# Self attention in a fused transformer kernel: from masked copies of the keys over 96 and 112 rows to one head per 32-partition row tile

## The chip, the cores and the metric

The kernel runs on one core of one Trainium2 chip. The metric is device time in microseconds (us) of one execution, median of several; lower is better. TensorE is written PE (its weight loads PEld), VectorE DVE, ScalarE ACT, GpSimd POOL, SyncE SP.

## What is computed

The reference runs four layers, each an attention and a feed-forward block, over x of 4 batches x 512 tokens x 128 channels. The change touches the last layer's self attention (16 heads of 8 channels, full 512 x 512, no mask), which stands in the fourth feed-forward block ahead of its routed experts:

```
h = layernorm(y)*g + b                        # y: 512 x 128 of one batch
q, k, v = h @ wq + bq, h @ wk + bk, h @ wv + bv
p = softmax(q_h @ k_h.T / sqrt(8))            # for each head h of 16, 512 x 512
y = y + concat_h(p @ v_h) @ wo + bo
then a layernorm, a router (top 1 of 8) and eight experts of 128 -> 512 -> 128
```

## The kernel before

One program drives five engines. For every engine a function (`tensor`, `scalar`, `vector`, `gpsimd`, `sync`) holds generators of the same names, and `order` (from L2350) interleaves the same streams in the same way for all five: `weave` advances the stream whose next piece has the earliest fractional time. Each engine executes its own list strictly in that order; semaphores (`Signal`, waits through `Waits`) tie the lists together. So a wait that stands in an engine's list holds back all that is behind it. PSUM has 8 banks of 512 words; `Banks.take` hands out banks of a ring, and the user of a bank waits for the reader of its last use.

The self attention (loop at L2403) has 16 units s, one for each batch b = s // 4 and group g = s % 4 of four heads. In turn i of 18 the streams are `first(i)`, `second(i-1)` and `third(i-2)`:

- `first` projects queries and keys of one group. The weights hold the 32 columns of the group three times, so a projection of 96 rows gives three copies. ACT adds the bias and rounds to float32r (L1134, L1118), DVE subtracts to get the low parts for one of the copies (L1500, L1486). With three copies (high, low, high against high, high, low) a float32r product keeps nearly float32 accuracy. Then DVE and ACT write four masked copies of the keys, 112 rows each (L1493, L1125, two each), so that a product over all rows sees one head alone.
- `second` finds the maximum of each query over its 512 keys: for 4 query blocks t and 2 head pairs, two products over 96 rows into banks 0 to 3 and one DVE reduction over two banks (L1884), 8 a unit. Four transposes (L516) turn the maxima into rows, DVE copies them (L1513), and SP moves them by one DMA (L2197) into rows 96 to 111 of the queries.
- `third` makes the scores transposed (keys on partitions) over 112 rows, the maximum subtracted through its row: 16 products with banks 4 to 6 as ring, 16 exponentials on ACT (L1325), and 4 groups of value products (`values`, 128 rows x 32 columns, four at a time, float32) into bank 7, copied to OT by DVE (L1897).

`third(s)` starts with `w.wait_ge(*mq[par].at("s", s))`, the landing of the maxima. Beside the units run `self_norms(b+1)` (two layernorms, the transposed and scaled h, values; turns 2, 6, 10), `tail4` (division by the sums, output projection; turns 6, 10, 14), `route3` (router, same turns) and `place3(0)` (slots of the experts; turn 11). All small pieces of these streams take their banks from the ring of 4 to 6 as well.

## Time and profile before

| | |
|---|---|
| median of 3 runs | 1301.2 us (1296.91 to 1304.37) |
| the profiled execution | 1300.78 us, its span 1299.0 us |
| PE, DVE, ACT, POOL busy | 1063.6, 691.8, 445.7, 139.2 us |
| mean granted TensorE clock | 0.875 |
| self attention, from the first raw products to the last output copy | about 821 to 1184 us of the span |

Busy time of an engine is the time in which it had at least one instruction under way; matmuls are pipelined, so their durations overlap. The granted clock is a share of full speed: 1.00 is 2.4 GHz, 0.50 is 1.2 GHz. A rate in brackets behind a timeline row is the idle time before it and who ended it.

### The profile page before, as it was taken

The numbers are of one execution on the slowest core, as the hardware profiler recorded it, in microseconds if no ns is written. First come the engines' busy times: TensorE is split into PE (matmuls) and PEld (weight loads), VectorE is DVE, ScalarE is ACT, GpSimd is POOL, SyncE is SP. The second block draws the span as 40 slices with busy tenths as digits, with TensorE's granted clock in tenths as the row PEclk, the third lists the DMA queues.
The fourth block names the chain that finished last, engine by engine and source line by source line (L and its number), as shares of the span: only waits on it lengthen the run. The fifth ranks groups of instructions, "written<-read, shape, count | busy, mean of one in ns | idle before, by whom it ended". The sixth has DMA issues, their size and how long they took to land.

```text
span 1299.0 us, 14949 instructions
## 1 busy us (share of the span) xinstructions
PE 1063.6 (82%) x5592; PEld 594.4 (46%) x5592; DVE 691.8 (53%) x1741; ACT 445.7 (34%) x834; POOL 139.2 (11%) x135
## 2 busy tenths in 40 slices
PE   4688999999977773875988888789789789898983
PEld 2244566665533332652753333344444444444753
DVE  5345656554554533327434434777767767673532
ACT  2334333232132220112223223356446336354431
POOL 1000000000001112015210001000100120000222
PEclk7889999999986865996888899789889879789987
DMA  9500000000210000121000000000000000001122
GB/s 297 161 1 1 1 1 1 1 1 1 77 54 1 7 6 27 44 65 25 2 6 1 1 1 1 2 2 3 2 3 3 2 17 3 1 2 33 41 62 71
DMA packets 31216, 33.34 MB, mean 26 GB/s; under 512 B 4037, under 2 KB 22621, under 8 KB 31144
## 3 DMA queue, kind: packets, MB, share of 16 engines
q1 hardware_dynamic: 29096, 28.59, 7.2%
q0 software_dynamic: 2048, 3.79, 1.1%
q8 instruction: 45, 0.74, 0.2%
q14 instruction: 27, 0.22, 0.1%
HBM read 22.53 MB, written 9.70 MB: 25 GB/s over the span
## 4 chain that ended last, share of the span: by engine, by line
PE 67%; DVE 21%; issue 5%; ACT 3%; POOL 2%; DMA 1%; SPq 0%; POOLq 0%; DVEq 0%; ACTq 0%
PE PS L170 61%; DVE MX L1884 5%; DVE KB L1555 3%; PE PS L634 2%; DVE KB L1493 1%; DVE Ht L1422 1%; DVE st L1409 1%; DVE OT L1596 1%; PE PS L1020 1%; PE PS L516 1%; DVE STG L1486 1%; POOL OT L2096 1%; PE PS L642 1%; POOL ve L2079 1%; DVE CX L1596 1%
## 5 line engine op out<-in xcount | busy, mean ns | idle before, releaser
L1325 ACT ACTIVATE PT<-PS 128x512 f32<-128x512 f32 x256 | 140.9, 596 | 114.1 <-PE PS L170 112.3
L1884 DVE TENSOR_REDUCE MX<-PS 128x2 fp32r<-128x1024 f32 x128 | 151.9, 1218 | 14.2 <-PE PS L170 13.2
L1220 ACT ACTIVATE PT<-PS 77x512 f32<-77x512 f32 x192 | 98.0, 590 | 158.5 <-PE PS L170 158.5
L170 PE MATMUL PS<-CX 32*77 32x512 f32 (+2 forms) x896 | 128.0, 579 | 18.9 <-DVE OT L1596 7.8
L170 PE MATMUL PS<-HT,RA 128*128 128x512 f32 x288 | 131.6, 599 | 0.0
L170 PE MATMUL PS<-KB,QB 96*128 96x512 f32 x256 | 102.5, 494 | 25.4 <-DVE MX L1884 23.3
L2079 POOL TENSOR_TENSOR ve<-ve,nh 128x4 f32<-128x4 f32 x40 | 41.4, 1036 | 699.6 <-DVE ve L1417 699.6
L170 PE MATMUL PS<-QB,KB 112*128 112x512 f32 x256 | 107.6, 473 | 3.0 <-ACT PT L1325 2.3
L1555 DVE TENSOR_REDUCE KB<-PS 128x16 fp32r<-128x1232 f32 x48 | 69.1, 1439 | 70.7 <-PE PS L170 70.4
L170 PEld LDWEIGHTS PS<-RA,PT 128*128 128x128 f32 x816 | 98.8, 193 | 16.2 <-issue 16.2
L170 PE MATMUL PS<-RA,PT 128*128 128x128 f32 (+1 forms) x816 | 102.8, 277 | 1.5 <-DVE PT L2006 1.2
L1254 ACT ACTIVATE PT<-PS 128x512 f32<-128x512 f32 x72 | 42.9, 597 | 127.7 <-PE PS L170 127.7
L170 PE MATMUL PS<-HT,S 128*96 128x512 f32 (+1 forms) x104 | 71.5, 782 | 14.2 <-DVE KB L1555 10.9
L170 PEld LDWEIGHTS PS<-KB,QB 96*128 96x128 f32 x256 | 48.0, 212 | 74.5 <-DVE MX L1884 48.6
L1723 DVE TENSOR_TENSOR PT<-PT,PS 128x512 f32<-128x512 f32 x72 | 49.5, 687 | 57.0 <-PE PS L170 48.1
L170 PEld LDWEIGHTS PS<-CX 32*128 32x128 f32 (+1 forms) x896 | 48.1, 191 | 66.7 <-issue 21.5
L170 PEld LDWEIGHTS PS<-HT,RA 128*128 128x128 f32 x288 | 52.3, 192 | 54.2 <-issue 53.3
L170 PE MATMUL PS<-PT,RB 128*32 128x512 f32 x512 | 71.8, 654 | 0.0
L170 PEld LDWEIGHTS PS<-QB,KB 112*128 112x128 f32 x256 | 49.9, 202 | 47.1 <-ACT PT L1325 35.5
L170 PE MATMUL PS<-PT,VB 77*32 77x512 f32 x384 | 57.7, 677 | 6.1 <-ACT CX L1168 3.2
L170 PE MATMUL PS<-KB 32*77 32x512 f32 x192 | 53.9, 960 | 0.0
L170 PE MATMUL PS<-RB,PT 128*128 128x128 f32 (+2 forms) x352 | 49.8, 303 | 4.2 <-DVE PT L1580 3.3
(236 smaller groups left out, 1363.5 us busy)
## 6 DMA issues: line engine op xcount, KB each, us to landing
RA<-in_l_w SPq DMA_DIRECT2D x1, 2304.0 KB, 11.0
RB<-in_l_w SPq DMA_DIRECT2D x1, 2048.0 KB, 14.2
RA<-in_l_w SPq DMA_DIRECT2D x1, 2048.0 KB, 8.7
d<-OT SPq DMA_DIRECT2D x2, 960.0 KB, 7.9
RB<-d SPq DMA_DIRECT2D x6, 256.0 KB, 3.1
o<-PT SPq DMA_DIRECT2D x6, 256.0 KB, 2.3
dbuf<-OT SPq DMA_DIRECT2D x2, 640.0 KB, 4.9
X<-in_x SPq DMA_DIRECT2D x4, 256.0 KB, 4.5
```

The lines of the kernel that those rows point to most:

```text
L170: return e.matmul(o, l, r, start=first, stop=last, skip_group_check=True)
L516: m = e.transpose(PS[0:M.shape[2], k, 128 * t:128 * t + 128], M[:, t, :].bitcast(F32), ident[:, :])
L634: m = e.transpose(PS[:, k, 128 * hg:128 * hg + 128], outputs_at(key, hg)[:, 128 * j:128 * j + 128], ident[:, :])
L642: m = e.transpose(PS[:, k, 128 * j:128 * j + 128], ON[:, 256 * j + 128 * c:256 * j + 128 * c + 128], ident[:, :])
L1220: e.activation(slot[s][0:NK, :], PS[0:NK, 4 + j, :], ACT.Exp, bias=0.0, scale=a.scale).then_inc(*expd(i, r, j))
L1254: e.activation(slot[s], PS[:, banks.of(silu, i, x, c), :], ACT.Silu).then_inc(*silu(i, x, c))
L1325: e.activation(slot[p], PS[:, banks.of(expd, "s", s, c, j), :], ACT.Exp, bias=0.0, scale=a4.scale).then_inc(*expd("s", s, c, j))
L1555: e.tensor_reduce(o, PS[:, 0:4, 0:308].rearrange("p i (r k) -> p i r k", k=NK), AX, ALU.max).then_inc(*rmax(i, t))
L1596: e.tensor_copy(outputs_at((i,), r), PS[:, 0, :]).then_inc(*otc(i, r))
L1723: e.tensor_tensor(P, P, PS[:, banks.of(glu, i, x, c), :], ALU.mult).then_inc(*glu(i, x, c))
L1884: e.tensor_reduce(Mv[par][:, t, RM + 4 * g + 2 * p2:RM + 4 * g + 2 * p2 + 2], PS[:, 2 * p2:2 * p2 + 2, :], AX, ALU.max).then_inc(*rmax("s" ...
L2079: e.tensor_tensor(ve[:, 8 * par + 4:8 * par + 8], ve[:, 8 * par:8 * par + 4], nh[:, :], ALU.pow).then_inc(*rstd(*key))
```

## The change

Each head of a group gets a row tile of 32 partitions: rows 0 to 7 of the tile hold the high part, 8 to 15 the low part, 16 to 23 the high part again (for the keys high, high, low), and row 24 the maximum (against -1 in the keys). So no masked copies are needed, and a product of one head uses 32 rows.

- Queries and keys of all 16 heads are projected once per batch, in `self_norms` (two 128 x 512 products), and split into high and low there (ACT, then DVE with 128 x 512). `first` puts the rows of a group in place with selector matrices (two accumulating float32r products over 128 rows for the queries, two for the keys), each followed by one ACT copy (QS, KS). The selectors are loaded (1 MB) and rounded once by POOL, after turn 21 of the earlier units.
- `second`: products over 32 rows, the two of a pair on neighbouring row tiles, into a pair of banks out of 0 to 3 (`take_pair`); the maxima are 16 columns, one transpose, one ACT copy of 16 x 128, and SP moves them by four DMAs of one row each.
- `third`: scores over 32 rows with banks 4 to 6; everything else now takes banks of 0 to 3. The output copy goes from DVE to ACT, one unit later in its list.
- `tail4`, `route3` and `place3(0)` are placed otherwise: `route3` in turns 7, 11, 15, `place3(0)` in turn 13.

```diff
@@ tensor: self_norms
+                for n, wt in enumerate((a4.wq, a4.wk)):
+                    k, free = banks.take(qsplit, "n", b, n)
+                    w.wait_ge(*free)
+                    mm(e, PS[:, k, :], wt, HTv[par]).then_inc(*projected("n", b, n))
+                    yield
@@ tensor: first
-                yield from queries(a4, ("s", b), b % 2, g, hT.at("s", b))
-                yield from keys(a4, s, g, 512, HTv[b % 2])
+                w.wait_ge(*pinit.at("sel"))
+                for n, (N, done) in enumerate(((QN[b % 2], qact), (KNv[b % 2], kact))):
+                    k, free = banks.take(done, "s", s)
+                    w.wait_ge(*free)
+                    w.wait_ge(*qsplit.at("n", b, n))
+                    mm(e, PS[:, k, :], SELm[:, 2 * n, g, :], N[0], True, False)
+                    mm(e, PS[:, k, :], SELm[:, 2 * n + 1, g, :], N[1], False, True).then_inc(*(kproj if n else projected)("s", s))
+                    yield
@@ tensor: second
-                        for j in range(2):
-                            k = 2 * p2 + j
-                            w.wait_ge(*banks.take_at(k, rmax, "s", s, t, p2))
-                            m = mm(e, PS[:, k, :], QQ[par][0:RM, 512 * g + 128 * t:512 * g + 128 * t + 128], kv[0:RM, 2 * p2 + j, :])
+                        k, frees = banks.take_pair(rmax, "s", s, t, p2)
+                        for free in frees:
+                            w.wait_ge(*free)
+                        for j in (2 * p2, 2 * p2 + 1):
+                            m = mm(e, PS[:, k + j % 2, :], Q[32 * j:32 * j + 32, 128 * t:128 * t + 128], K[32 * j:32 * j + 32, :])
                         m.then_inc(*raw("s", s, t, p2))
                         yield
-                yield from maxima(("s", s), Mv[par], rmax.at("s", s, 3, 1))
+                k, free = banks.take(mts, "s", s)
+                w.wait_ge(*free)
+                w.wait_ge(*rmax.at("s", s, 3, 1))
+                e.transpose(PS[0:16, k, 0:128], MXs[s % 2].bitcast(F32), ident[:, :]).then_inc(*mxT("s", s))
@@ tensor: third, scores
-                        k, free = banks.take(expd, "s", s, c, j)
-                        w.wait_ge(*free)
-                        mm(e, PS[:, k, :], kv[0:RK, j, 128 * c:128 * c + 128], QQ[par][0:RK, 512 * g:512 * g + 512]).then_inc(*scored("s", s, c, j))
+                        k = 4 + (4 * c + j) % 3
+                        w.wait_ge(*banks.take_at(k, expd, "s", s, c, j))
+                        mm(e, PS[:, k, :], K[32 * j:32 * j + 32, 128 * c:128 * c + 128], Q[32 * j:32 * j + 32, :]).then_inc(*scored("s", s, c, j))
@@ scalar: first, second, third
+                e.activation(QS[s % 4], PS[:, banks.of(qact, "s", s), :], ACT.Copy).then_inc(*qact("s", s))
+                e.activation(KS[s % 4], PS[:, banks.of(kact, "s", s), :], ACT.Identity, bias=a4.minus, scale=1.0).then_inc(*kact("s", s))
+                w.wait_ge(*mxT.at("s", s))
+                e.activation(MTs[s % 2][0:16, :], PS[0:16, banks.of(mts, "s", s), 0:128], ACT.Copy).then_inc(*mts("s", s))
+                    e.activation(OT[:, 512 * g:512 * g + 512], PS[:, 7, :], ACT.Copy).then_inc(*ots("s", b, g))
@@ sync: second
-                e.dma_start(QQ[par][RM:RK, 512 * g:512 * g + 512].bitcast(F32), MT[RM:RK, :].bitcast(F32)).then_inc(*mq[par]("s", s))
+                for j in range(4):
+                    e.dma_start(QS[s % 4][32 * j + 24:32 * j + 25, :].rearrange("o (t q) -> o t q", t=4).bitcast(F32),
+                                MTs[s % 2][4 * j:4 * j + 4, :].bitcast(F32)).then_inc(*mq[s % 2]("s", s))
@@ order
-                    streams.append((first(i), 12))
+                    streams.append((first(i), [0.1, 0.16]))
-                    streams.append((second(i - 1), 11))
+                    streams.append((second(i - 1), [0.12 * n for n in range(9)]))
-                    streams.append((tail4((i - 6) // 4), 36))
+                    streams.append((tail4((i - 6) // 4), 14, 0.3))
-                if i in (6, 10, 14):
-                    streams.append((route3((i - 6) // 4), 22, 0.4))
-                if i == 11:
+                if i in (7, 11, 15):
+                    streams.append((route3((i - 7) // 4), 26))
+                if i == 13:
```

How the lists of two engines change is shown at two places. First PE, where a unit's maxima are transposed and the next unit's scores begin, in a turn without other streams. L516 and L883 are the transposes of the maxima; KB,QB are raw products, QB,KB scores, PT,RB value products, HT,S the old query projection, QB,RR the new selector products. Before:

```order
L516 MATMUL PS<-ident,MX 112x128 [waits rmax,expd]
L516 MATMUL PS<-ident,MX 112x128 x3
L170 MATMUL PS<-QB,KB 128x512 [waits expd] x2
L170 MATMUL PS<-PT,RB 32x512 x4
L170 MATMUL PS<-PT,RB 32x512 [waits expd]
L170 MATMUL PS<-PT,RB 32x512 x3
L170 MATMUL PS<-HT,S 96x512
L170 MATMUL PS<-KB,QB 128x512 [waits kcD,kcA]
L170 MATMUL PS<-KB,QB 128x512 x3
L170 MATMUL PS<-QB,KB 128x512 [waits mq0]
```

Now:

```order
L177 MATMUL PS<-PT,RB 32x512 x4
L177 MATMUL PS<-PT,RB 32x512 [waits expd]
L177 MATMUL PS<-PT,RB 32x512 x3
L883 MATMUL PS<-ident,KB 16x128 [waits rmax]
L177 MATMUL PS<-KB,QB 128x512 [waits mts]
L177 MATMUL PS<-KB,QB 128x512
L177 MATMUL PS<-QB,RR 128x512 x2
L177 MATMUL PS<-QB,KB 128x512 [waits mq1]
L177 MATMUL PS<-KB,QB 128x512 [waits qact]
```

The transpose moved behind the last value products of the unit before, and one pair of raw products instead of two stands between it and the first score.

Second ACT at the same place (L1302 and L1325 are the exponentials, L1293 the copy of the maxima, L1282 and L1286 the copies of queries and keys, L1309 the output copy). Now:

```order
L1302 ACTIVATE PT<-PS 128x512 [waits scored] x3
L1293 ACTIVATE KB<-PS 16x128 [waits mq1,mxT]
L1282 ACTIVATE QB<-PS 128x512 [waits projected]
L1302 ACTIVATE PT<-PS 128x512 [waits scored,weighed]
L1302 ACTIVATE PT<-PS 128x512 [waits scored]
L1286 ACTIVATE KB<-PS,cols 128x512 [waits kproj]
L1302 ACTIVATE PT<-PS 128x512 [waits scored] x2
L1309 ACTIVATE OT<-PS 128x512 [waits weighed]
L1302 ACTIVATE PT<-PS 128x512 [waits scored] x4
```

Before, in the like turn:

```order
L1325 ACTIVATE PT<-PS 128x512 [waits scored,weighed]
L1325 ACTIVATE PT<-PS 128x512 [waits scored]
L1118 ACTIVATE STG<-PS,cols 96x512 [waits kcA,kcD,kproj]
L1325 ACTIVATE PT<-PS 128x512 [waits scored] x2
L1325 ACTIVATE PT<-PS 128x512 [waits scored,weighed]
L1125 ACTIVATE KB<-STG,msk 112x512 [waits ksplit]
L1125 ACTIVATE KB<-STG,msk 112x512
L1325 ACTIVATE PT<-PS 128x512 [waits scored] x3
```

The copy of the maxima and the output copy are new in ACT's list; the copies of the keys' mask are gone.

## Rows read from the trace of the kernel before

**Rows 1.** Groups by line, 861.7 to 1183 us: engine, count, busy, mean, idle before.
```profile
L1884 DVE TENSOR_REDUCE MX<-PS 128x2 fp32r<-128x1024 f32 x112 | 132.7, 1218 | 11.5 <-PE PS L170 10.7
L1325 ACT ACTIVATE PT<-PS 128x512 f32<-128x512 f32 x240 | 131.9, 597 | 103.0 <-PE PS L170 101.4
L170 PE MATMUL PS<-QB,KB 112*128 112x512 f32 x240 | 100.3, 471 | 3.0 <-ACT PT L1325 2.3
L170 PE MATMUL PS<-KB,QB 96*128 96x512 f32 x224 | 87.1, 480 | 17.9 <-DVE MX L1884 17.9
```

**Rows 2.** Stretches: length, busy PE, PEld, DVE, ACT, POOL, clock, DMA share, GB/s.
```profile
815.00:861.70 46.70, 34.61 (x120) 17.37 (x121) 34.94 (x62) 17.13 (x29) 3.47 (x3) 0.78 0.01 2
895.60:912.50 16.90, 15.60 (x73) 7.14 (x74) 13.08 (x14) 11.03 (x20) 0.00 (x0) 1.00 0.01 3
912.50:946.30 33.80, 25.66 (x124) 13.89 (x124) 25.23 (x72) 13.52 (x23) 5.76 (x5) 0.90 0.01 1
946.30:970.50 24.20, 20.98 (x89) 10.86 (x90) 14.79 (x21) 11.62 (x21) 0.00 (x0) 0.86 0.01 2
...
1039.30:1069.20 29.90, 25.14 (x91) 13.02 (x92) 19.85 (x42) 11.62 (x21) 8.68 (x8) 0.71 0.06 19
1103.10:1133.60 30.50, 26.43 (x112) 13.60 (x111) 18.87 (x41) 12.55 (x22) 2.31 (x2) 0.78 0.01 2
...
1157.90:1172.00 14.10, 13.70 (x69) 6.69 (x70) 10.56 (x10) 8.37 (x16) 0.00 (x0) 1.00 0.02 6
1172.00:1183.00 11.00, 10.16 (x49) 3.36 (x50) 0.69 (x1) 8.16 (x16) 0.00 (x0) 1.00 0.15 44
```

**Rows 3.** Timeline of the end of a turn without other streams: start, duration, what.
```profile
892.02 2.28 ACT L1325 ACTIVATE PT<-PS 128x512 f32<-128x512 f32 x4 [1.11 <-PE PS L170]
892.12 0.62 PE L516 MATMUL PS<-ident,MX 128*112 128x128 f32 x4
...
893.50 0.51 SPq L2197 DMA_DIRECT2D QB<-MT  x1
893.60 1.92 PE L170 MATMUL PS<-PT,RB 128*32 128x512 f32 x16
...
895.59 0.69 DVE L1897 COPY OT<-PS 128x512 f32<-128x512 f32 x1 [2.11 <-PE PS L170]
```

**Rows 4.** Groups by line, 860 to 1240 us: work of a unit beside reductions and exponentials.
```profile
L1125 ACT ACTIVATE KB<-STG,msk 112x512 fp32r<-112x512 f32 x26 | 17.2, 711 | 0.0
...
L1493 DVE TENSOR_SCALAR KB<-STG,msk 112x512 fp32r<-112x512 f32 x26 | 13.7, 570 | 0.3
...
L1513 DVE CAST MT<-PS 16x512 fp32r<-16x512 f32 x14 | 9.8, 697 | 10.0 <-PE PS L516 9.9
L1486 DVE SCALAR_TENSOR_TENSOR STG<-PS,cols,STG 32x512 fp32r<-32x512 f32 x13 | 9.7, 749 | 0.8 <-ACT STG L1118 0.4
```

**Rows 5.** Tile QB, 861 to 905 us: durations min, median, max in ns; landing of DMAs.
```profile
L170 PE MATMUL PS<-QB,KB x42: 389/397/645, 863.4 to 904.3; 112*128 112x512 f32 x42
...
DMA to landing us min/median/max: 1.9/1.9/1.9
```

**Rows 6.** Timeline of SP's queue: two issues with two others between them.
```profile
21.16 0.39 SPq L2176 DMA_DIRECT2D MT<-in_mbT  x1
...
22.35 0.33 SPq L2176 DMA_DIRECT2D off<-in_c_off  x1
```

**Rows 7.** Stretches of 3 us within a heavy turn, columns as in Rows 2.
```profile
929.00:932.00 3.00, 0.45 (x2) 0.00 (x1) 2.90 (x10) 2.30 (x4) 1.01 (x1) 1.00 0.00 0
932.00:935.00 3.00, 2.37 (x7) 1.58 (x7) 3.00 (x8) 0.10 (x1) 1.44 (x1) 0.52 0.00 0
```

**Rows 8.** Timeline: one group of value products at either clock.
```profile
885.57 1.07 PE L170 MATMUL PS<-PT,RB 128*32 128x512 f32 x8
...
937.63 1.69 PE L170 MATMUL PS<-PT,RB 128*32 128x512 f32 x8
```

**Rows 9.** Timeline: four float32r products of 32 rows in an earlier attention.
```profile
754.39 0.81 PE L170 MATMUL PS<-KB 32*77 32x512 f32 x4
```

More of the change, by code:

```diff
@@ L23 @@
 NT = 15
-RM = 96
-RK = 112
 GATE = 25
@@ L91, in again, with only @@
     def again(self):
-        self.order, self.ends = list(self.places), {}
-    def only(self, places):
-        self.order = list(places)
+        self.order, self.ends, self.paired = list(self.places), {}, False
+    def only(self, places, paired=False):
+        self.order, self.paired = list(places), paired
     def hold(self, k):
@@ L110, in take, with take_pair @@
     def take(self, signal, *key):
-        k = self.order.pop(0)
+        alone = [k for k in self.order if k ^ 1 not in self.order] if self.paired else []
+        k = (alone or self.order)[0]
+        self.order.remove(k)
         self.order.append(k)
         return k, self.take_at(k, signal, *key)
+    def take_pair(self, signal, *key):
+        k = [k for k in self.order if k ^ 1 in self.order][0] & 6
+        self.order = [x for x in self.order if x & 6 != k] + [k, k + 1]
+        frees = [self.take_at(k + n, signal, *key) for n in (1, 0)]
+        return k, frees
     def of(self, signal, *key):
@@ L180, in program @@
         KB = sb("KB", 3 * 2048, F32R)
+        with nc.sbuf_tensor("RR", [128, 8192], F32R) as RRt:
+            RR = RRt
         RB = sb("RB", 8192)
@@ L238, in program @@
         vall = VB[:, :].rearrange("p (b h c) -> p b h c", b=4, h=16)
-        Mv = [MX[:, 4 * RK * p:4 * RK * p + 4 * RK].rearrange("p (t c) -> p t c", t=4) for p in range(2)]
         W13 = RA[:, 0:9 * 512].rearrange("p (e n) -> p e n", e=9)
@@ L489, in prepare @@
                     banks.free(k)
-            def keys(a, n, g, cols_n, rhs):
-                k, free = banks.take(ksplit, n)
-                w.wait_ge(*free)
-                mm(e, PS[0:96, k, 0:cols_n], a.wk[:, g, :], rhs).then_inc(*kproj(n))
-                banks.hold(k)
-                yield from idle(2)
-                banks.free(k)
-                yield from idle(2)
-            def queries(a, key, par, g, ready):
-                k, free = banks.take(qsplit, *key, g)
-                w.wait_ge(*free)
-                w.wait_ge(*ready)
-                w.wait_ge(*ld[a.ready].all())
-                mm(e, PS[0:96, k, :], a.wq[:, g, :], HTv[par]).then_inc(*projected(*key, g))
-                banks.hold(k)
-                yield from idle(2)
-                banks.free(k)
-                yield
-            def maxima(key, M, ready):
-                k, free = banks.take(mtc, *key)
-                w.wait_ge(*free)
-                w.wait_ge(*ready)
-                for t in range(4):
-                    m = e.transpose(PS[0:M.shape[2], k, 128 * t:128 * t + 128], M[:, t, :].bitcast(F32), ident[:, :])
-                m.then_inc(*mxT(*key))
-                banks.hold(k)
-                yield
-                banks.free(k)
-                yield
             def front(i):
@@ L912, in values @@
                     if c == 0:
-                        w.wait_ge(*banks.take_at(7, otc, "s", b, g))
+                        w.wait_ge(*banks.take_at(7, ots, "s", b, g))
                         w.wait_ge(*vprep.at("s", b))
@@ L1054, in hook @@
                 elif name == "self":
-                    banks.only([4, 5, 6])
+                    banks.only(range(4), True)
                 elif name == "experts3":
@@ L1332, in third @@
                     yield
+                if s == 15:
+                    outputs(s)
             def tail4(b):
@@ L2126, in self_norms @@
                 add_row(Yb[b], 4, ("s", b))
-                yield
+                yield from idle(3)
             def tail4(b):
@@ L2164, in hook @@
                     gather(1)
+                elif name == "l3x1":
+                    w.wait_ge(*ld["l3sel"].all())
+                    e.tensor_copy(RR[:, 6144:8192], RB[:, 6144:8192]).then_inc(*pinit("sel"))
             nothing = lambda *a: none()
@@ L2282, in hook @@
                     w.wait_ge(*capV.at("o", 7))
-                    load("l3s", w4, A["l3s_w"])
+                    load("l3s", w4[:, 0:512], A["l3s_w"])
                 elif name == "l2m":
@@ L2289, in hook @@
                     load("c3", C3[:, 0:368], A["c_3"])
+                    w.wait_ge(*pe2.at(19, "down"))
+                    load("l3sel", RB[:, 6144:8192], A["l3_sel"])
             nothing = lambda *a: none()
@@ L2493 @@
         msk[:, 36 + n] = part // 16 == n
+    sel = _np.zeros((4, 4, 128, 128), _np.float32)
+    for g in range(4):
+        for j in range(4):
+            for k, places in enumerate(((0, 2), (1,), (0, 1), (2,))):
+                for n in places:
+                    for d in range(8):
+                        sel[k, g, 32 * g + 8 * j + d, 32 * j + 8 * n + d] = 1.0
     place8 = _np.arange(128).reshape(4, 4, 8).transpose(1, 0, 2).ravel()
```

201 lines of the change are left out of this document (69 added, 132 removed).

## The prediction

> **What bounds the kernel now.** I read the busy shares first (PE 1063.6 of 1299 us), then stretches turn by turn, then the timeline of one turn, because the average says nothing about this stage. The output copy of each unit (L1897) marks the turns. In a turn without other streams the stretch is 16.9 us [rows 2]: PE is busy 15.6 us of it, at full clock, DVE 13.1, ACT 11.0. I call this a plain turn; there are seven in the stage (3, 4, 5, 8, 9, 12, 13), all at 16.9 us. In the whole stage ACT idled 103 us ahead of its exponentials, 101.4 of it for PE [rows 1]. So plain turns are bound by PE's list. The heavy turns are another matter: turn 6, with two layernorms, the output tail and the router, lasts 33.8 us with DVE busy 25.2 and PE 25.7 [rows 2]; turn 7 lasts 24.2, turn 11 29.9, turn 14 30.5. There DVE's load and the waits between engines decide, and PE falls to the lower clock: after three microseconds with PE busy 0.45 us, the next three had a granted clock of 0.52, close to the 1.2 GHz level [rows 7].
>
> The change promises PE time: raw products and scores cost PE 87.1 and 100.3 us in this stretch [rows 1]. What replaces PE as the bound must be read from the order lists, and there I find a chain, below.
>
> **A plain turn after the change.** I walk from the first exponential of a unit to the first of the next.
>
> (a) ACT. Four exponentials back to back took 2.28 us [rows 3], so 16 take 9.1. Between them stand the copy KS and the output copy, 128 x 512 like an exponential (0.60 us mean, [rows 1]) and with a bias somewhat more: 1.3 together. The score bank ring has three banks, so ACT has up to three exponentials ahead while PE makes value products (1.07 us a group, [rows 8]), and a score product after them takes 0.40 [rows 5]; three exponentials are 1.7 us. That just covers it; I add 0.2 for joints. Sum 10.6 us. QS is copied in the pause (b).
>
> (b) The way back. By the order list all is serial now: last exponential of the unit, last value products (1.1 us), transpose of the maxima (0.35, from four in 0.62 [rows 3]), ACT's copy of 16 x 128 (0.3; bounds: 0.2 and the 0.70 of the 16 x 512 copy it replaces [rows 4]), SP's four DMAs, landing, the wait of the first score, the score itself (0.4), start of ACT (0.1). A DMA of this kind landed 1.9 us after its issue [rows 5]. Four issues of small loads in a row are 0.40 us apart (21.16 to 22.35 us holds three gaps, [rows 6]), so the last lands 1.2 + 1.9 = 3.1 us after the copy; with signals between engines 3.3. Sum: 1.1 + 0.35 + 0.3 + 3.3 + 0.5 = 5.55 us. In this time PE has one raw pair and one selector pair, under 1.2 us, and everything behind the score waits in its list: raw products too, so DVE gets one reduction of eight.
>
> Before, the transposes stood four scores, value groups and a projection ahead: the DMA left at 893.50 while PE still had the 1.92 us of values at 893.60 and raw products after them [rows 3], so it was covered. The one DMA, a copy on DVE and this cover are what the change gives up.
>
> (c) Together 10.6 + 5.55 = 16.2 us at full clock. DVE needs 13.1 less two masked copies (2 x 0.57), the transposed maxima 0.70, two splits (2 x 0.75) [rows 4] and the output copy 0.69 [rows 3], so 9.1 to 9.4 us: hidden. PE needs about 11: hidden too, but see the clock.
>
> (d) The clock. Over the last 3.6 us of the way back PE is busy about 1.1 us. [Rows 7] show such a lull followed by the 1.2 GHz level. There the value group took 1.69 instead of 1.07 us [rows 8], and the first score after it comes late by twice that and more, past the three exponentials in store: about 1.3 us for a chunk. If every lull is followed by some 6 us at the low level, one chunk and the first score are hit: +1.4 us, 17.6 us. If the whole turn runs there, two chunks (2.6), the last values (0.9 + 0.6) and the start: +4.5, 20.7 us. I take 17.6. The Trainium skill ("TensorE: Matmul & The Clock Gate", section "HAM oscillation") says that PE-idle gaps between bursts let the gate throttle again and that each burst then starts cold, which would make the 20.7 likelier than the 16.2; no row here shows this pattern for 32-row products.
>
> **The other turns**, before and after:
> - Turns 6, 10. DVE 25.2 us [rows 2], less 4.0 of the unit's work, less the router's layernorm that moves out (2.6), plus the two 128 x 512 splits of the batch (1.5): 20.1. DVE idled 8.6 of the turn before; now it must idle in the way back, 5.55 less one reduction, and a little for POOL. About 26 against 33.8: -15.6 for two.
> - Turns 7, 11, 15 (router). DVE about 14 to 14.6, again with a pause of 4.4 and joints: 20.5 against 24.2, 29.9 [rows 2] and, for 15, about 24.2: -16.8.
> - Turn 14 loses the router: 20 against 30.5 [rows 2]: -10.5.
> - Turn 13 is plain plus `place3` (about 20 small DVE pieces): 19 against 16.9: +2.1.
> - Six plain turns, 17.6 against 16.9: +4.2.
> - Turns 16 and 17 have no new raw products to hide and were short, 14.1 and 11.0 [rows 2]. They hold the same chain: 17 and 15: +6.9.
> - The start (turns 0 to 2, 46.7 us from 815, [rows 2]): no masks ahead of the first product, raw pairs on two row tiles so that DVE's reductions follow each other at 1.22, less DVE in turn 2, but two more projections and splits in `self_norms(0)`: -5, between -10 and 0.
> - Elsewhere: the selector load (1 MB) and POOL's rounding (about four times the 1.3 us of its 128 x 512 operations) have some 130 us until the first use, and POOL is 11% busy: 0. The experts start from the same point: 0.
>
> Sum: -15.6 - 16.8 - 10.5 + 2.1 + 4.2 + 6.9 - 5 = -34.7 us. The profiled execution took 1300.8, 0.4 under the median; 1266 us, which I give for both.
>
> **Rivals.**
> 1. *The clock stays high* or heavy turns shrink further. For: plain turns before ran at 1.00, and the pause is broken by a raw pair and selectors. Against: [rows 7]. It gives 16.2 in seven plain turns (-10) and 1 us less in nine others: about 1247.
> 2. *The whole stage at 1.2 GHz, slower than before.* The mechanism: every way back drops the clock, and at the low level value products (1.69, [rows 8]) outlast the exponentials in store, so that PE is thin and slow for the whole turn. Plain turns 20.7: +3.1 on seven, +2.5 on nine others: 1266 + 44 = 1310. It decides for slower from about 2 us a turn over my values. Against: PE dense again in each turn should bring the clock back, as it did within some 6 us after [rows 7].
> 3. *A longer way back*: four one-row DMAs cost more than 0.40 apart, or land later. 0.5 us more a step and 0.6 more landing give 1.5 + 0.6 = 2.1 us, of which turns 6 and 10 hide some: 14 x 2 = 28: 1294.
> 4. *Nothing gained*: the heavy turns keep their length because waits, not DVE work, made them (DVE idled 8.6 us there). Then -42.9 of the sum shrinks to some -10: about 1299.
> 5. *PE's saving comes through whole.* Four row tiles at once: four 32-row products took 0.81 us under way together [rows 9] where a 112-row one takes 0.40 alone [rows 5]. Three quarters of 87.1 + 100.3 us [rows 1] are 141 us: 1160. The Trainium skill ("TensorEngine Tiling (Array Packing)", section "Theoretical Speedup") puts up to 4x on products of 32 rows or fewer, which is this sum. Against: the scores are fed one by one by exponentials of 0.57 us, and the pause in (b) is not PE work. That the change makes no 32-row tiles is excluded by its operands.
>
> **How the numbers follow.** Forecast as summed (1250 to 1283): 0.50. Rival 1: 0.22. Rival 3: 0.12. Rival 2: 0.08. Rival 4: 0.06. Rival 5: 0.02. Half a per cent (6.5 us), about what a measurement of this kernel can tell from no change, puts the lines at 1294.7 and 1307.7. Faster: 0.50 + 0.22 + 0.02 + a good half of rival 3 and a little of 4, 0.83. Within: the rest of 3 and 4 and some of rival 2, 0.09. Slower: 0.08. The range takes in rivals 1, 3 and 4: 1236 to 1300; the unknown prices (DMA spacing, ACT's small copy, the start) fit in it. The predicted time is the forecast's.
>
> **What would show it.** Right: plain turns 16 to 18 us between output copies, in each a stretch near 5.5 us where ACT does only the small copy and QS, PE's first score waiting for the DMA; reductions waiting for PE; granted clock dipping behind each pause; PE busy well under 1063 us; turn 6 about 26 us. Wrong: plain turns near 12 us would mean the pause is covered; over 19 us, rival 2 or 3, told apart by the granted clock and by the time from the small copy to the landing; turn 6 still over 31 us, rival 4.

## The result and the profile after

The changed kernel took 1374.72 us (median of 4 runs, 1366.99 to 1383.11) against 1302.78 for the kernel before (median of 4 runs, 1296.91 to 1309.14): a ratio of 1.055, 95% interval 1.046 to 1.065. It is slower by 5.5%. The forecast was 1266 us, its range 1236 to 1300, and slower had a chance of 0.08. The profiled execution took 1367.5 us, its span is 1364.9 against 1299.0 before, so 65.9 us have to be found.

The page of the changed kernel: its busy line and the granted clock in 40 slices. The mean clock is 0.784 (0.875 before).

```profile
PE 1097.2 (80%) x5560; PEld 573.9 (42%) x5560; DVE 638.1 (47%) x1651; ACT 441.1 (32%) x842; POOL 140.4 (10%) x136
...
PEclk7799999999977757968887896757556655757987
```

PE has 33.6 us more busy time (1063.6 before), though the products of this stage are smaller, and the slices of the self attention, from the 26th to the 37th, read 5 to 7.

The groups by line from 869.2 to 1250.5 us, which answer to [rows 1] (columns as there):

```profile
L1836 DVE TENSOR_REDUCE KB<-PS 128x2 fp32r<-128x1024 f32 x110 | 134.0, 1225 | 155.4 <-PE PS L177 155.3
L1302 ACT ACTIVATE PT<-PS 128x512 f32<-128x512 f32 x237 | 127.7, 600 | 144.0 <-PE PS L177 143.4
L177 PE MATMUL PS<-QB,KB 32*128 32x512 f32 x236 | 113.7, 725 | 39.8 <-DMA QB<-KB 31.2 <-ACT PT L1302 8.6
L177 PE MATMUL PS<-PT,RB 128*32 128x512 f32 x480 | 104.9, 990 | 0.3 <-ACT PT L1302 0.3
L177 PE MATMUL PS<-KB,QB 32*128 32x512 f32 x220 | 94.8, 692 | 11.5 <-ACT KB L1293 4.6 <-DVE rt L1856 3.0 <-DVE KN L1822 1.1
```

DVE and ACT work as long as before on each reduction and exponential (1225 and 600 ns against 1218 and 597), and wait longer, for PE. A mean score product (QB,KB) lasts 725 ns where the 112-row product took 471, a mean raw product (KB,QB) 692 where the 96-row product took 480. The value products, which the change does not touch, went from a mean of 650 to 990 ns; their line in the kernel before, 861.7 to 1183 us:

```profile
L170 PE MATMUL PS<-PT,RB 128*32 128x512 f32 x480 | 66.7, 650 | 0.0
```

The wait for the DMA of the maxima is there too, 31 us in the whole stage; the experiments below tell how much of the loss it makes.

The stretches between output copies (now L1309 on ACT), columns as in [rows 2]: the start, two plain turns (3 and 4), turns 6, 7, 11, 14, 15, 16, 17 and the experts behind them.

```profile
815.00:869.20 54.20, 39.48 (x158) 18.65 (x154) 32.64 (x64) 18.56 (x34) 3.29 (x3) 0.71 0.00 1
869.20:891.30 22.10, 19.53 (x73) 6.32 (x70) 9.86 (x9) 10.42 (x22) 0.00 (x0) 0.50 0.01 1
891.30:913.30 22.00, 18.65 (x71) 5.99 (x69) 9.72 (x9) 10.32 (x22) 0.00 (x0) 0.58 0.00 0
934.60:967.90 33.30, 25.89 (x117) 12.20 (x116) 19.10 (x49) 14.20 (x27) 4.57 (x4) 0.76 0.00 1
967.90:1000.60 32.70, 26.58 (x97) 11.52 (x96) 12.38 (x21) 11.20 (x23) 0.00 (x0) 0.50 0.00 1
1077.10:1109.80 32.70, 26.54 (x97) 11.57 (x97) 12.28 (x21) 11.15 (x22) 0.00 (x0) 0.50 0.00 1
1153.80:1183.70 29.90, 22.68 (x101) 10.31 (x100) 14.66 (x30) 12.12 (x23) 2.32 (x2) 0.73 0.01 1
1183.70:1215.50 31.80, 24.01 (x93) 10.47 (x93) 12.62 (x21) 9.79 (x20) 0.00 (x0) 0.55 0.00 1
1215.50:1236.70 21.20, 15.98 (x60) 4.79 (x59) 6.85 (x6) 8.95 (x19) 0.00 (x0) 0.58 0.08 25
1236.70:1250.50 13.80, 12.13 (x44) 2.81 (x44) 0.00 (x0) 6.73 (x14) 0.00 (x0) 0.50 0.00 1
1250.50:1364.90 114.40, 82.74 (x508) 61.32 (x508) 44.51 (x140) 34.97 (x88) 26.58 (x26) 0.90 0.18 54
```

A plain turn takes 22.0 us where it took 16.9, with the clock at 0.50 to 0.58, that is at the 1.2 GHz level for nearly all of it. ACT's and DVE's busy times, 10.4 and 9.8 us, are near what the forecast had. What changed is PE: it is busy 18.7 to 19.5 us, where the forecast had about 11.

Stretches of 3 us inside one such turn, same columns:

```profile
894.30:897.30 3.00, 2.69 (x16) 0.84 (x15) 1.04 (x1) 1.41 (x3) 0.00 (x0) 0.50 0.00 0
897.30:900.30 3.00, 3.00 (x14) 0.66 (x13) 1.32 (x2) 0.95 (x3) 0.00 (x0) 0.50 0.00 0
900.30:903.30 3.00, 2.69 (x13) 0.89 (x15) 2.45 (x2) 1.78 (x4) 0.00 (x0) 0.50 0.00 0
903.30:906.30 3.00, 2.64 (x15) 0.47 (x7) 0.00 (x0) 0.27 (x1) 0.00 (x0) 0.60 0.00 0
906.30:909.30 3.00, 0.98 (x4) 0.30 (x2) 1.23 (x1) 0.60 (x1) 0.00 (x0) 0.97 0.01 3
909.30:912.30 3.00, 2.67 (x8) 1.08 (x8) 1.23 (x1) 1.77 (x3) 0.00 (x0) 0.50 0.00 0
```

The second row is what the forecast did not foresee: PE is busy 3.00 of 3.00 us and the clock is at 0.50. The clock comes up in the pause, right behind the 16 value products, and is down again when the next unit begins. These rows alone do not say whether the pause or the products after it bring the clock down; the experiments have to. The Trainium skill ("TensorE: Matmul & The Clock Gate", section "What's actually happening") says that the gate is set by how busy PE has been recently. If busy is read as the profile's busy time, this row speaks against it.

The timeline of the same turn's end (start, duration, what):

```profile
897.25 1.94 PE L177 MATMUL PS<-PT,RB 128*32 128x512 f32 x8
...
901.80 3.64 PE L177 MATMUL PS<-PT,RB 128*32 128x512 f32 x16
905.37 0.38 PE L883 MATMUL PS<-ident,KB 128*16 128x128 f32 x1
906.11 0.50 PE L177 MATMUL PS<-KB,QB 32*128 32x512 f32 x2 [0.36 <-ACT KB L1293]
906.54 0.73 PE L177 MATMUL PS<-QB,RR 128*128 128x512 f32 x2
909.59 0.79 PE L177 MATMUL PS<-QB,KB 32*128 32x512 f32 x1 [2.32 <-DMA QB<-KB]
909.60 0.80 PE L177 MATMUL PS<-KB,QB 32*128 32x512 f32 x2
...
910.32 1.22 PE L177 MATMUL PS<-KB,RR 128*128 128x512 f32 x2
```

The value group takes 1.94 us (1.07 at full clock, [rows 8]). SP's four DMAs were issued from 906.09 on, and the first score, at 909.59, waits for the last of them, as foreseen. Two raw products on neighbouring row tiles took 0.80 us together at the low level, about as long as one alone, where a pair over 128 rows took 1.22.

### The profile page after: what moved, and what is told of

It is laid out like the page before. It is cut to its first block, busy times and chain, and to the rows that moved or that the text cites. A ratio compares the mean times of both kernels' runs of the same rounds, so it can differ in the third digit from the quotient of the medians.

```text
span 1364.9 us, 14813 instructions
## 1 busy us (share of the span) xinstructions
PE 1097.2 (80%) x5560; PEld 573.9 (42%) x5560; DVE 638.1 (47%) x1651; ACT 441.1 (32%) x842; POOL 140.4 (10%) x136
## 4 chain that ended last, share of the span: by engine, by line
PE 69%; DVE 13%; ACT 5%; issue 5%; DMA 3%; POOL 2%; SPq 2%; POOLq 0%; ACTq 0%; DVEq 0%
PE PS L177 62%; DVE KB L1505 3%; PE PS L608 3%; ACT PT L1302 2%; SPq L2142 2%; DMA QB<-KB 2%; DVE KB L1836 1%; DVE Ht L1407 1%; DVE OT L1546 1%; POOL ve L2021 1%; PE PS L1008 1%; DVE st L1394 1%; POOL OT L2038 1%; DVE CX L1546 1%; PE PS L616 1%
## 5 line engine op out<-in xcount | busy, mean ns | idle before, releaser
L1836 DVE TENSOR_REDUCE KB<-PS 128x2 fp32r<-128x1024 f32 x128 | 155.6, 1224 | 169.9 <-PE PS L177 169.7
L1302 ACT ACTIVATE PT<-PS 128x512 f32<-128x512 f32 x256 | 138.1, 599 | 154.5 <-PE PS L177 153.8
L177 PE MATMUL PS<-QB,KB 32*128 32x512 f32 x256 | 122.9, 719 | 43.8 <-DMA QB<-KB 35.1
L177 PE MATMUL PS<-KB,QB 32*128 32x512 f32 x256 | 107.8, 689 | 18.0 <-ACT KB L1293 5.3
L177 PE MATMUL PS<-PT,RB 128*32 128x512 f32 x512 | 110.7, 980 | 0.3 <-ACT PT L1302 0.3
L177 PEld LDWEIGHTS PS<-QB,KB 32*128 32x128 f32 x256 | 51.1, 277 | 137.5 <-issue 53.7
L177 PEld LDWEIGHTS PS<-KB,QB 32*128 32x128 f32 x256 | 41.9, 273 | 35.6 <-ACT KB L1293 9.1
L177 PE MATMUL PS<-HT,S 128*128 128x512 f32 x56 | 42.8, 865 | 15.5 <-DVE KB L1505 10.8
```

What stands on the lines that cost most here:

```text
L177: return e.matmul(o, l, r, start=first, stop=last, skip_group_check=True)
L1302: e.activation(slot[p], PS[:, banks.of(expd, "s", s, c, j), :], ACT.Exp, bias=0.0, scale=a4.scale).then_inc(*expd("s", s, c, j))
L1836: e.tensor_reduce(o, PS[:, k:k + 2, :], AX, ALU.max).then_inc(*rmax("s", s, t, p2))
```

## The experiments

Two theories ran through the first four runs. Theory A is the forecast's mechanism: the pause in each way back lowers the clock. Theory B, called N in the later runs: products that use only 32 rows leave the clock low even where PE is busy without a gap. The kernel before, run on the same chips, took 1303.3 to 1307.5 us. Runs without an interval are single executions.

**The pause covered.** The second stream begins its steps earlier, so that the transpose stands before the last score and two value groups.

```
-    streams.append((second(i - 1), [0.12 * n for n in range(9)]))
+    streams.append((second(i - 1), [0.1 * n for n in range(9)]))
```

> The changed kernel with the raw products of a unit placed at 0.1 n of a turn instead of 0.12 n, so that the transpose of the maxima stands before the last score and two value groups. The changed kernel's plain turn is 22.0 us, of which the pause from the last values to the first score is about 4.2 us. Theory A (the pause both costs its own length and drops the clock): the pause is covered, plain turns fall to 13 to 16 us with a granted clock of 0.9 or more in them, the kernel to 1250 to 1290 us. Theory B (32-row products do not bring the clock up, whatever stands between them): the pause goes, but the granted clock stays near 0.5, plain turns 17.5 to 19 us, kernel 1315 to 1340 us.

It took 1351.5 us. PE no longer waits for the DMA of the maxima. Six of the seven plain turns were 20.5 to 21.4 us at a clock of 0.50 to 0.64, one was 16.7 at 0.81. The turn lost at most 1.5 us, not the clock's share: the direction of theory B, though slower than its figures (17.5 to 19 us, 1315 to 1340 us).

**The pause filled.** The two selector products for the queries are made four times, so that PE works with 128 rows in the pause.

```
+    for _ in range(FILL if n == 0 else 0):
+        mm(e, PS[:, k, :], SELm[:, 2 * n, g, :], N[0], True, False)
+        mm(e, PS[:, k, :], SELm[:, 2 * n + 1, g, :], N[1], False, True)
```

> The changed kernel with the two selector products of the queries made four times instead of once (same result), in the pause ahead of the first score, so that PE works there on all 128 rows. The order of everything else is kept. Theory A (the idle pause drops the clock): the clock stays or comes up, the value groups take 1.07 instead of 1.94 us, plain turns 17 to 18.5 us, kernel 1315 to 1335 us. Theory B (the 32-row products leave the clock low): the clock rises at most for the start of the unit and falls again; plain turns 20 to 22 us, kernel 1350 to 1375 us.

1377.2 us, plain turns 20.9 to 22.8 us at 0.57 to 0.67, slightly above theory B's figures in time. PE's wait for the DMA was down to 0.94 us in turns 4 and 5, and the first score behind it took 0.50 us, as at full clock, where the changed kernel's took 0.79. The mean clock of the turn rose by less than 0.1 for it: work over 128 rows in the pause does not hold the clock up through the unit.

**One DMA in place of four.**

```
-    for j in range(4):
-        e.dma_start(QS[s % 4][32 * j + 24:32 * j + 25, :]...)
+    e.dma_start(QS[s % 4][24:128:32, :].bitcast(F32), MTs[s % 2][0:16, :].bitcast(F32)).then_inc(*mq[s % 2]("s", s))
```

> The changed kernel with the four one-row DMAs of a unit's maxima as one DMA to partitions 24, 56, 88 and 120. The issues took 2.42 us for four; with one the landing comes 1.5 to 1.9 us earlier in each of 16 turns. If the way back is a serial chain: 24 to 30 us less, 1340 to 1350 us, and with a shorter lull perhaps a higher clock and more. If the landing is not what the first score waits for: no change, 1367 to 1383 us.

1355.9 us, some 12 us under the changed kernel's profiled run (the fastest but one of its four runs, which spread from 1367.0 to 1383.1), and half of the 24 to 30 us expected: plain turns 18.3 to 21.2 us, still at 0.50 to 0.72. So the way back is on the path, and its four issues cost about 0.6 us each, but it is a small part of the loss.

**A pause in the kernel before.** Its transposes are moved behind the last value products.

```
-    streams.append((second(i - 1), 11))
+    streams.append((second(i - 1), [n / 11 for n in range(9)] + [0.96, 0.97, 0.98]))
```

> The kernel before, with its four transposes of the maxima moved behind the last value group of the unit before, as in the changed kernel; nothing else is changed. It adds a pause of about 2.5 us (DMA of 1.9 us less the products in between). Theory A (a pause drops the clock): plain turns go from 16.9 to above 21 us with clock 0.5 to 0.7 in them, kernel 1345 us or more. Theory B (products over 96 and 112 rows hold the clock, only 32-row ones do not): plain turns 19 to 20 us at clock 0.95 or more, kernel 1325 to 1345 us.

1312.4 us against 1304.9 for the kernel before on that chip. Plain turns took 18.2 to 18.3 us (two 19.9) and kept a clock of 1.00 (those two 0.91). That is less than either theory had (19 to 20 us, or over 21), because the pause made was small: PE waits 1.05 to 1.12 us for the DMA, where the changed kernel's waits 2.3 in most plain turns. Such a pause costs 1.3 us a turn and lowers the clock in two of seven. It is a weak test of theory A; the next run has the full pause.

**Full rows in the changed kernel.** The next four runs change how many rows the products contract and, so that all values stay finite, the scale of the exponentials. They compute something else than the reference. In this one both kinds of products use all 128 rows.

```
-    ...Q[32 * j:32 * j + 32, 128 * t:128 * t + 128], K[32 * j:32 * j + 32, :])
+    ...Q[:, 128 * t:128 * t + 128], K[:, :])
-    ...K[32 * j:32 * j + 32, 128 * c:128 * c + 128], Q[32 * j:32 * j + 32, :])
+    ...K[:, 128 * c:128 * c + 128], Q[:, :])
-    ...ACT.Exp, bias=0.0, scale=a4.scale)
+    ...ACT.Exp, bias=0.0, scale=0.01 * a4.scale)
```

> Leaves the computation changed: the raw and score products contract all 128 rows (the four heads of a tile at once), with the exponentials' scale cut to a hundredth so that all stays finite; the number of instructions, their columns and their order are the changed kernel's. Theory N (the granted clock follows the rows that the products use, so that products of 32 rows alone leave it at 1.2 GHz even where PE is busy without a gap): plain turns at a granted clock of 0.90 to 1.00 and 16.5 to 18.5 us long, 1265 to 1300 us in all. Rival O (the clock stays low for the order of the work or its waits, not for its rows): the clock stays at 0.50 to 0.60, plain turns 21 to 22.5 us, 1360 to 1380 us.

1312.3 us, beside 1307.5 for the kernel before on the same chip: 55 us under the changed kernel's profiled run (62 under its median), most of the loss. A plain turn and its 3 us stretches, in this run:

```profile
889.96:906.93 16.97, 13.96 (x70) 7.03 (x69) 9.68 (x9) 10.40 (x21) 0.00 (x0) 1.00 0.00 0
...
892.00:895.00 3.00, 3.00 (x20) 1.58 (x16) 1.82 (x3) 2.35 (x6) 0.00 (x0) 1.00 0.00 0
...
901.00:904.00 3.00, 0.71 (x3) 0.30 (x2) 1.23 (x1) 0.60 (x1) 0.00 (x0) 1.00 0.01 3
904.00:907.00 3.00, 2.64 (x12) 1.80 (x10) 1.31 (x2) 2.69 (x6) 0.00 (x0) 1.00 0.00 0
```

The way back is still there: PE is busy 0.71 of 3 us, and here the clock stays at 1.00 in it and after it. Five of the seven plain turns read 1.00. The other two do not:

```profile
906.93:925.16 18.23, 15.58 (x69) 8.11 (x68) 12.03 (x21) 10.53 (x21) 1.02 (x1) 0.85 0.01 1
...
1091.47:1111.29 19.82, 16.02 (x71) 8.13 (x69) 13.04 (x21) 10.52 (x21) 8.29 (x8) 0.83 0.08 27
```

In each a wait for the maxima (2.28 us in the first) is followed by three microseconds at 0.50. So it is in the turns with side streams: of the 14 waits from turn 3 on, five are followed by three microseconds at 1.00, nine by three at 0.50 to 0.77. Theory A's mechanism is there, then, and costs a plain turn 1.3 us when it strikes (18.23 for 16.97). But with full rows the clock comes back within the next turn, and with 32 rows it comes up for a few microseconds at most in nearly every turn; that is what keeps the changed kernel's turns low. Theory B's figures for the plain turn are met in five turns of seven, its total (1265 to 1300 us) is missed by 12 us. The raw and the score products, by duration in two turns of each kernel (minimum, median, maximum in ns), of the changed kernel:

```profile
L177 PE MATMUL PS<-KB,QB x34: 490/789/792, 868.5 to 912.3; 32*128 32x512 f32 x34
L177 PE MATMUL PS<-QB,KB x34: 623/788/792, 869.1 to 913.0; 32*128 32x512 f32 x34
```

and with all rows:

```profile
L177 PE MATMUL PS<-QB,KB x34: 388/396/503, 872.8 to 907.0; 128*128 128x512 f32 x34
...
L177 PE MATMUL PS<-KB,QB x32: 389/393/501, 873.5 to 906.5; 128*128 128x512 f32 x32
```

Four times the rows, half the time.

**Full rows in the scores alone, and in the raw products alone.** The second or the first of the two edits above, with the smaller scale in both.

> The score products alone contract all 128 rows, the raw products stay at 32; the exponentials' scale is cut to a hundredth. Scores are half of the narrow columns (16 products of 512 a turn) and lie beside the value products in ACT's stretch. Theory N: the clock is up in ACT's stretch and low in the raw stretch or in none: mean 0.75 to 1.00 in plain turns, 17 to 19.5 us, 1280 to 1325 us. Rival O: 0.50 to 0.60, 21 to 22.5 us, 1360 to 1380 us.

> The raw products alone contract all 128 rows, the scores stay at 32; the exponentials' scale is cut to a hundredth. Theory N: half way too, as with the scores alone: clock 0.70 to 1.00 in plain turns, 17 to 20 us, 1285 to 1335 us. Rival O: 0.50 to 0.60, 21 to 22.5 us, 1360 to 1380 us.

Scores alone: 1374.2 us, plain turns 19.3 to 26.4 us at 0.56 to 0.85. Raw products alone: 1429.7 us, 20.9 to 28.2 us at 0.56 to 0.83. Both missed theory B's half way figures in time, and the raw products' run is slower than the rival had it too. The clock did rise above the changed kernel's, for some turns, but not to stay. That these runs are slower than the changed kernel at a higher clock may come from 128-row products taking their full time at the low level where two 32-row products lie side by side; it was not tried apart. Both runs use the smaller scale of the exponentials and are slow, so that edit alone does not bring the clock back.

**32 rows in the kernel before.** The converse: its raw and score products cut to the first 32 rows, nothing else but the scale.

```
-    ...QQ[par][0:RM, ...], kv[0:RM, 2 * p2 + j, :])
+    ...QQ[par][0:32, ...], kv[0:32, 2 * p2 + j, :])
-    ...kv[0:RK, j, ...], QQ[par][0:RK, ...])
+    ...kv[0:32, j, ...], QQ[par][0:32, ...])
```

> The kernel before, its raw and score products cut from 96 and 112 rows to the first 32, so that they leave out most of each product (the maximum too; the exponentials' scale is cut to a hundredth); instructions, columns, order and waits are the kernel's before. Theory N: the clock falls to 0.50 to 0.65 in the plain turns, which then take 20 to 22.5 us, 1350 to 1400 us in all. Rival O: the clock stays at 0.95 to 1.00, plain turns 16.5 to 17.5 us, 1295 to 1310 us.

1405.9 us, theory B's direction and beyond its figures (1350 to 1400 us, plain turns of 20 to 22.5). Plain turns went from 16.9 us to 25.7 (one 23.4, one 20.3) at clocks of 0.56 to 0.83. All its narrow products lie on rows 0 to 31, so none can lie beside another on a different row tile. Four stretches of 3 us where the clock falls:

```profile
863.90:866.90 3.00, 2.61 (x9) 1.20 (x9) 2.00 (x3) 1.27 (x3) 0.00 (x0) 1.00 0.00 0
866.90:869.90 3.00, 3.00 (x10) 1.50 (x10) 2.97 (x3) 1.91 (x5) 0.00 (x0) 0.98 0.00 0
869.90:872.90 3.00, 3.00 (x10) 1.35 (x12) 2.51 (x4) 2.49 (x5) 0.00 (x0) 0.50 0.01 3
872.90:875.90 3.00, 3.00 (x12) 1.48 (x5) 2.17 (x4) 0.10 (x2) 0.00 (x0) 0.50 0.00 0
```

There is no pause as in the changed kernel, PE is busy 2.61 of 3 us and then throughout, and the clock drops to 1.2 GHz. The kernel before held 1.00 with the same instructions in the same order on 96 and 112 rows. With the run on all rows this settles from both sides that the rows of these products decide.

It does not make a rule for every 32-row product. An earlier attention of the kernel before has four heads on four row tiles, its products of 32 rows among others of 77. Two stretches of it:

```profile
692.00:695.00 3.00, 3.00 (x28) 1.21 (x23) 1.61 (x6) 2.04 (x4) 0.00 (x0) 1.00 0.00 0
...
722.00:725.00 3.00, 3.00 (x20) 1.05 (x16) 1.62 (x5) 0.00 (x0) 0.00 (x0) 0.50 0.00 0
```

PE is busy 3.00 of 3 us in both, and the clock is at the upper level in one and at the lower in the other. Whether four tiles under way at once would hold the clock in the self attention, and whether the number of rows or the change between products of 32 and of 128 rows is what counts, was not tried.

**What full clock and a covered way back would give.** Full rows, the earlier second stream and one DMA together.

> As wide_both (products over all 128 rows, so another computation; the clock came back with it), and also the second stream at tenths of the turn and one DMA in place of four, so that the way back of the maxima lies beside score and value products. With the clock at 1.00 the 2.3 us in which PE waits for the row of maxima should go: theory N with a serial way back: plain turns 14.3 to 15.2 us at 0.95 to 1.00, 1260 to 1290 us in all. Rival: the way back, or ACT's and DVE's copies for the selectors, still ends after the products, and another wait takes its place: plain turns 16 to 17 us, 1295 to 1315 us.

1301.5 us beside 1306.8 for the kernel before. The clock stays at 1.00 in the six plain turns, the DMA wait is gone, and such a turn takes 17.0 to 17.3 us all the same: the rival held. PE's timeline of such a turn:

```profile
898.07 0.27 PE L883 MATMUL PS<-ident,KB 128*16 128x128 f32 x1 [0.95 <-DVE KB L1836]
...
902.23 0.73 PE L177 MATMUL PS<-KB,QB 128*128 128x512 f32 x2 [0.69 <-ACT QB L1282]
...
905.00 0.73 PE L177 MATMUL PS<-KB,QB 128*128 128x512 f32 x2 [0.89 <-ACT KB L1286]
```

The transpose now waits for the last reduction (0.95), and raw products wait for the banks that the selector products fill and ACT empties (0.69 and 0.89). The turn is a ring of short waits as long as the list it replaced. What the covered way back gives against full rows alone is 10.8 us (1312.3 to 1301.5), mostly in the router's turns 7, 11 and 15: 24.8, 22.8 and 20.2 us at 0.90 to 1.00, where they had 26.0, 27.1 and 28.1 at 0.74 to 0.87.

**The same two edits on the changed kernel itself.**

> The changed kernel, its result untouched, with the second stream at tenths of the turn and one DMA in place of four. Each alone gave 1351.5 and 1355.9 against 1367.5. Theory N: the way back is gone as a wait, but products of 32 rows still keep the clock at 0.50 to 0.65, so the turn is PE's busy time, 18.3 to 20.5 us, and the kernel takes 1335 to 1352 us. Rival: the gap in PE was what let the clock fall, and four DMAs in a row kept part of it in the run with the early second stream: clock over 0.80, plain turns near 17 us, under 1320 us.

1343.2 us, as theory N said: plain turns 20.3 to 20.7 us at 0.58 to 0.63. Two took 16.7 and 16.8 us at 0.81 and 0.80, the rival's figures; so the clock can stay up for part of a turn of 32-row products, and what decides it there is open. This is the best of the changed kernel's versions, 3% over the kernel before.

**The moved side streams alone.** The kernel before with routing in turns 7, 11 and 15, the tails early in their turn, the placing in turn 13.

```
-    streams.append((tail4((i - 6) // 4), 36))
+    streams.append((tail4((i - 6) // 4), 14, 0.3))
-if i in (6, 10, 14):
-    streams.append((route3((i - 6) // 4), 22, 0.4))
-if i == 11:
+if i in (7, 11, 15):
+    streams.append((route3((i - 7) // 4), 26))
+if i == 13:
```

> The kernel before with only the change's moves of the side streams (routing into turns 7, 11, 15, the tails early in their turn, the placing of tokens in turn 13); all products as before. Theory N puts the whole slowdown on the products' rows, so these moves are harmless: turns 6 and 7 together 56 to 58 us as before (58.0), 1290 to 1308 us. If the moves carry the gain that the prediction had put on turns 6, 7, 10, 11 and 14: 1260 to 1285 us. Rival S (the new schedule itself costs): 1315 to 1330 us.

1305.8 us (10 runs), ratio 0.999, 95% interval 0.997 to 1.002. The total is as expected, turns 6 and 7 together are not: 63.0 us for 56 to 58. Turns 6 and 10 fell from 33.8 and 34.9 us to 31.2 and 26.8, turns 7 and 11 rose from 24.3 and 29.9 to 31.8 and 32.9. The time moved with the router. Turns 14 and 15 did the same (30.6 and 24.3 to 22.3 and 30.2), and turn 13 grew by 6.9 us. The forecast had put 42.9 us on these heavy turns; the move brings nothing of it.

**Routing later in its turn.** The same with one number more.

```
-    streams.append((route3((i - 7) // 4), 26))
+    streams.append((route3((i - 7) // 4), 26, 0.3))
```

> The kernel before with the moved side streams, and routing begun 0.3 of a turn later. In the run with the moved streams turn 7 took 31.8 us, of which PE waited some 6 us for VectorE's and ScalarE's routing steps, and its clock fell to 0.73. If routing beside the later raw and score products finds more of PE's work to lie beside: turns 7 and 11 27 to 29.5 us, 1290 to 1298 us. Rival: the chain of small steps holds the turn wherever it starts: 31 to 33 us, 1302 to 1312 us.

1292.2 us (4 runs), ratio 0.989, 95% interval 0.984 to 0.995. This is 1.1% under the kernel before and the fastest of all versions. Turns 7 and 11 in the run before and in this one:

```profile
943.54:975.33 31.79, 25.76 (x101) 14.07 (x102) 17.95 (x40) 12.38 (x22) 1.02 (x1) 0.73 0.01 2
...
1036.00:1068.92 32.92, 28.84 (x101) 15.35 (x102) 17.95 (x39) 12.39 (x22) 1.02 (x1) 0.64 0.00 1
```

```profile
947.42:971.16 23.74, 19.42 (x93) 10.05 (x94) 17.57 (x39) 12.51 (x22) 1.02 (x1) 0.93 0.01 2
...
1034.44:1059.57 25.13, 20.82 (x93) 11.04 (x94) 17.56 (x38) 12.52 (x22) 1.02 (x1) 0.86 0.01 1
```

The turns are 8 us shorter with DVE's busy time nearly the same, eight of PE's instructions go over to the next turn (18.0 us), and the clock holds up better. The gain in those turns is larger than expected. In this execution turn 2 ended at 867.1 us, against 861.7 in the kernel before and 861.5 in the run before; nothing ahead of turn 6 differs from that run, so this is spread between executions and no cost of the edit. Later routing without the move to another turn was not tried.

## Why the prediction was wrong

The terms of its sum against the profiled runs, in us of difference to the kernel before. The last column is the changed kernel with full rows, where most of the clock is back.

| term | forecast | measured | full rows |
|---|---|---|---|
| six plain turns | +4.2 | +29.1 | +1.4 |
| turn 13 | +2.1 | +5.1 | +2.9 |
| turns 6, 10 | -15.6 | -2.2 | -6.3 |
| turns 7, 11, 15 | -16.8 | +18.8 | +2.8 |
| turn 14 | -10.5 | -0.7 | -4.8 |
| start, turns 16, 17 | +1.9 | +17.4 | +11.9 |
| experts | 0 | -1.6 | +3.6 |
| sum | -34.7 | +65.9 | +11.5 |

- **Step (d), the clock, failed, and with it the sign.** It took the clock to be lowered by the lull, for a chunk, gave it +1.4 us a turn, and priced the case that the whole turn runs low at +4.5 us (20.7) without taking it. The plain turn took 22.0 us, +5.1, at a mean clock of 0.50 to 0.58. What it had wrong is that the clock comes back by itself after a lull, whatever products follow. The runs showed that with 32-row products it does not, or not to stay: it is low in most turns when the lull is covered or filled, five of seven plain turns are at 1.00 when the same products use all rows with the lull left in, and it falls in the kernel before, without such a lull, when its products use 32. The forecast's own part, as read from [rows 7], holds with full rows: nine of 14 lulls were followed by the low level, a plain turn hit by it took 18.2 us for 17.0, near the +1.4 forecast, and covering the lulls gave 10.8 us in all. The price of 32 rows against full ones is 1367.5 - 1312.3 = 55 us, most of the 66.
- **Rival 2** named the outcome, 1.2 GHz in the whole stage, but through the lulls, and argued against itself with the step that failed: its "PE dense again in each turn should bring the clock back" is what the 3.00 of 3.00 us at 0.50 contradicts. At 1310 it was also 65 us short, because it took the plain turns at 20.7 us and the turns with side streams to lose 2.5 us each. At the low level PE is busy 24.0 to 26.6 us in turns 7, 11 and 15, and these take 31.8 to 32.7. The rule of the Trainium skill ("TensorE: Matmul & The Clock Gate", section "HAM oscillation") that a burst behind a PE-idle gap starts cold, which the forecast had weighed, would have raised the rival with the right outcome; the trace with full rows agrees with it after nine of 14 waits, but it is not what kept the whole turn low.
- **Step (a)**, 10.6 us from the first exponential of a unit to the last: 11.1 with full rows (887.30 to 898.38). **Step (b)**, 5.55 us: 5.9 there (898.38 to 904.28). The chain is the one described, and its terms are close. The four issues are 0.57 us each where [rows 6] gave 0.40, but the landing behind the last one was quicker, so from the first issue to the first score it is 3.50 (3.3 forecast). The value products end 1.3 us after the last exponential (1.1 forecast), the small copy was 0.27 (0.3). **Step (c)**: 16.97 us for 16.2. With full rows at full clock the plain turn is what it was, 16.9.
- **PE's load** was called about 11 us and hidden. With full rows it was 14.0; no turn of 32-row products at full clock was seen, so what they would take there stays open.
- **Turns 6 and 10** were read from DVE's busy time, 20.1 us (measured 19.1) plus the way back. They took 31.3 and 31.0 with full rows even at clocks of 0.92, with DVE idle for 12 of them: waits between engines made them, as rival 4 said. The step's own sum, 20.1 plus 5.55 less a reduction of 1.2, is 24.5 and leaves 1.5 us for POOL to reach its 26; and it took turn 10 at 33.8 where the trace has 34.9. **The router's turns**, forecast at 20.5, took 26.0 to 28.1 with full rows. The run with the moved streams alone shows the same: time moved from turn to turn, none was saved.
- **The start and turns 16, 17** stand in one row because the mark moved: L1309 now comes behind the first four exponentials of the next unit. With full rows it starts 8.5 us after the unit's last exponential (898.38 to 906.93), before it was 1.3 us (894.30 to 895.59), so some 7 us of the start's stretch belong to the end. Put back, full rows give about +4 for the start and +8 for the two last turns, against -5 and +6.9, so the end was right. Of the start's row, though, 8.4 us were there before the self attention began: the last value product of the earlier attention starts at 817.76 in that run and at 809.37 in the kernel before (814.17 in the changed kernel). From there on the start is about 4 us shorter, near the forecast. What makes the 8.4 us is open. Two runs with the same work up to there, the two with moved side streams, differ by 5.6 us at the end of turn 2, so part of it can be spread.
- **Rival 5**, at 0.02, was rightly small. 32-row products on different row tiles do overlap (a raw pair in 0.80 us at the low level, where a 128-row pair took 1.22), but the lower clock takes that back. Its 1160 us did not follow from its row: four products in 0.81 us against four times 0.40 are half, not a quarter, which gives some 94 us less, about 1207.

## What to carry to other kernels

When a change cuts the rows that products contract, price the whole stage at the lower clock as a likely case, not as a mishap, before crediting any overlap of row tiles. The trace of the kernel before had 32-row products at both levels, so reading it would have raised the question and not settled it; one run that changes the rows and nothing in the order did. A stage with several engines in a ring has to be read from its waits: DVE's busy time fell from 25.2 to 19.1 us in turn 6 and the turn stayed as long. A lull and a change of rows can both lower the clock, so a test that takes away one leaves the other to be tested. Moving a chain of small steps to another turn gave nothing; starting it later in that turn as well (one number more) gave 1.1%.

## What the runs showed of the hardware

- PE busy in the profile does not say at which clock it will run. With 128 rows per product the clock stayed at 2.4 GHz in five of seven plain turns, even through stretches with PE busy 0.71 of 3 us. With 32 rows it fell to 1.2 GHz with PE busy 3.00 of 3. The same instruction list gave 16.97 us a turn with 128 rows and 22.0 with 32; the kernel before gave 16.9 with 96 and 112 rows and 25.7 with 32. In an earlier attention, with 32-row products on four row tiles among others of 77 rows, both levels occur.
- With 128-row products, waits of PE of 1.9 to 3.9 us for a DMA were followed by three microseconds at 0.50 to 0.77 in nine of 14 cases and at 1.00 in five.
- Mixed rows did not give a mixed clock that pays: with only the scores or only the raw products on all rows the turns were up to 26.4 and 28.2 us long.
- Four DMAs of one row each, issued one after the other, took 2.42 us of SP's queue where one DMA of the four rows took 0.52, and the kernel 11.6 us less (1367.5 to 1355.9, single executions).
